# Two copies per tile for the first 24 tiles of the first expert layer, and an order that TensorE no longer reads

## The reference

```python
x = x + _L0_ffn_ref(_L0_cond_ref(x, fside, len, ...), gate_w, gate_b, w1, b1, w2, b2)
x = x + _L1_ffn_ref(_L1_cond_ref(x, W1, b1, v, type), gate_w, w_gate, w_up, w_down, ...)
# _L0_ffn_ref: 24 experts, each token takes its best 2
h = gelu(einsum('bsd,edf->besf', x, w1) + b1)        # 128 -> 512
y = einsum('besf,efd->besd', h, w2) + b2             # 512 -> 128
out = einsum('bse,besd->bsd', combine, y) + x
```

## Time and profile before

| | |
|---|---|
| three runs | 435.76, 437.19, 439.93 us, median 437.19 |
| the profiled execution | 436.51 us, its span 434.7 us, granted TensorE clock 0.942 |
| PE busy | 372.5 us (86%) |
| DVE busy | 281.0 us (65%) |
| ACT busy | 247.2 us (57%) |
| POOL busy | 198.7 us (46%) |
| attention | up to about 176 us |
| first expert layer | 176 to 275 us |
| second layer | 275 us to the end |

### The profile page before, as it was taken

How to read it: one execution, slowest core, us unless ns; L and a number is a source line. 1 busy time by engine, 2 the same in 40 slices (tenths; PEclk the granted TensorE clock), 3 DMA queues, 4 the chain that set the end, 5 groups by cost and what they waited for, 6 DMA issues and landing times.

```text
span 434.7 us, 10203 instructions
## 1 busy us (share of the span) xinstructions
PE 372.5 (86%) x2635; PEld 268.8 (62%) x2635; DVE 281.0 (65%) x1114; ACT 247.2 (57%) x742; POOL 198.7 (46%) x270
## 2 busy tenths in 40 slices
PE   3699999999999995399999899559988879999920
PEld 2356656666666653299999899226556547777710
DVE  3766787887887888366666466369575626666615
ACT  1288888788888783255665456237975114444400
POOL 3551143444433444634454555422747606666630
PEclk9999999999999997599999999759999989999975
DMA  7400999987777703366766676050111122323217
GB/s 153 76 15 13 315 355 228 242 185 165 176 193 188 141 15 98 93 171 177 200 172 182 176 191 193 17 185 15 50 37 44 56 51 78 90 76 82 68 46 248
DMA packets 61072, 57.14 MB, mean 131 GB/s; under 512 B 6042, under 2 KB 49703, under 8 KB 60768
## 3 DMA queue, kind: packets, MB, share of 16 engines
q1 hardware_dynamic: 56288, 48.10, 44.4%
q0 software_dynamic: 4736, 8.47, 5.8%
HBM read 36.12 MB, written 21.73 MB: 133 GB/s over the span
## 4 chain that ended last, share of the span: by engine, by line
PE 70%; DVE 7%; DMA 7%; issue 4%; ACT 3%; POOL 3%; SPq 2%; DVEq 1%; POOLq 0%; ACTq 0%
PE bank L735 13%; PE bank L863 8%; PE bank L1062 7%; PE bank L868 7%; PE bank L744 6%; PE bank L758 5%; PE bank L1079 2%; PE bank L1070 2%; PE bank L1080 2%; DMA w<-in_L_ffn_w_dram 2%; POOL layer_rows L703 2%; DMA qexp<-layer_outputs 2%; PE bank L788 2%; PE bank L774 1%; PE bank L838 1%
## 5 line engine op out<-in xcount | busy, mean ns | idle before, releaser
L1107 ACT ACTIVATE ps<-bank,ntop 128x128 f32<-128x128 f32 x256 | 73.6, 379 | 12.9 <-DVE ntop L1367 12.9
L1174 ACT ACTIVATE hT<-bank,w 128x128 f32<-128x128 f32 x176 | 51.0, 369 | 43.8 <-PE bank L863 43.4
L735 PE MATMUL bank<-qexp 128*128 128x512 f32 x128 | 67.7, 611 | 3.2 <-POOL qexp L645 2.7
L715 POOL DMA_INDIRECT layer_outputs<-w_all x40 | 38.9, 972 | 34.1 <-issue 20.4
L744 PEld LDWEIGHTS bank<-ident,ps 128*128 128x128 f32 x256 | 31.9, 141 | 33.3 <-issue 29.6
L863 PE MATMUL bank<-xT,w 128*128 128x128 f32 x352 | 49.3, 285 | 2.7 <-DMA w<-in_L_ffn_w_dram 1.2
L642 POOL TENSOR_TENSOR qexp<-kA,rowmask 128x512 f32<-128x512 f32 x16 | 16.6, 1039 | 73.2 <-DVE kA L1451 73.2
L1116 ACT ACTIVATE pT<-bank 128x512 f32<-128x512 f32 x64 | 38.6, 603 | 19.7 <-PE bank L744 18.4
L1366 DVE TENSOR_REDUCE mx<-bank 128x4 f32<-128x512 f32 x64 | 43.7, 683 | 7.5 <-PE bank L735 6.2
L863 PEld LDWEIGHTS bank<-xT,w 128*128 128x128 f32 x352 | 44.4, 198 | 4.7 <-issue 3.9
L703 POOL DMA_INDIRECT layer_rows<-rows_all,places x32 | 30.9, 966 | 23.8 <-DVE rows_all L1733 9.4
(11 more groups left out here) (312 smaller groups left out, 811.2 us busy)
## 6 DMA issues: line engine op xcount, KB each, us to landing
w<-in_L_ffn_w_dram SPq DMA_DIRECT2D x44, 258.0 KB, 3.4
layer_rows<-fill SPq DMA_DIRECT2D x10, 910.0 KB, 9.1
w_all<-in_L_ffn_w_dram SPq DMA_DIRECT2D x24, 256.0 KB, 5.1
qexp<-layer_outputs SPq DMA_DIRECT2D x8, 512.0 KB, 4.8
xt<-layer_rows SPq DMA_DIRECT2D x45, 65.0 KB, 2.5
w_all<-layer_rows SPq DMA_DIRECT2D x40, 65.0 KB, 1.8
xfT<-in_xfT_dram SPq DMA_DIRECT2D x16, 128.0 KB, 2.8
layer_rows<-fill SPq DMA_DIRECT2D x1, 1560.0 KB, 11.3
```

Source lines behind the costliest of these rows:

```text
L715: g.indirect_dma_start(ys1_dram, bass.IndirectOffsetOnAxis(ap=xt1[r][:, P:P + 1].bitcast(U32), axis=0), yb1[r][:, :], None, bounds_check=Y ...
L735: pe.matmul(psA[g % 2][:, :], qexp[b % 2][:, g, :], kexp[b % 2].rearrange("p g k -> p (g k)"), start=True, stop=True).then_inc(a_in_ps, 1)
L1107: m = s.activation(ps[g % 2][:, t, :], psA[g % 2][:, t * P:(t + 1) * P], ACT.Exp, bias=ntop[:, h:h + 1])
L1174: s.activation(hT[r % 2][:, c, :], banks[c][:, 0:P], ACT.Gelu, bias=w1[r][:, F0 + c:F0 + c + 1]).then_inc(gelu_done, 1)
```

## The change

DVE now copies w2 and b2 of the first 24 tiles too, with the same `keep_weights`, after take_xT(j+1) and ahead of the rest of iteration j. TensorE reads the four fixed buffers in every tile and loads no order word. DVE loads one word at every fourth tile, inside the loop, in place of all six ahead of it. The wait for all down weights (`w2_in`) moves from TensorE to DVE. In the second layer two waits are added: `pooled_rows(k)` on `pnT_ready`, `keep_pnT(k)` on `pl_in_ps`.

```diff
@@ tensor
-            pe.wait_ge(w2_in, 16 * E0)
-            pe.wait_ge(order_ready, 1)
-            words0 = [order_word(pe, n) for n in range(E0 // RING)]
+            def down_kept(j, r):
+                pe.wait_ge(weights_kept, 2 * j + 1)
+                down(j, r, lambda c: w2_r[r][:, c * P:(c + 1) * P])
+
             transpose_tile(0, 0, 0)
...
-                    down(j - 1, (j - 1) % RING, w2_ordered(j - 1))
+                    down_kept(j - 1, (j - 1) % RING)
...
             def pooled_rows(k):
+                pe.wait_ge(pnT_ready, k + 1)
@@ scalar
             def keep_pnT(k):
                 act.wait_ge(pn_in_ps, k + 1)
                 if k >= 1:
+                    act.wait_ge(pl_in_ps, k)
@@ vector
+            def keep_weights(e, r):
+                v.tensor_copy(w2_r[r], w2_all[:, bass.ds(e, 1), :].rearrange("p o f -> p (o f)")).then_inc(weights_kept, 1)
+                v.tensor_copy(b2_r[r], b2_all[:, bass.ds(e, 1), :].rearrange("p o d -> p (o d)")).then_inc(weights_kept, 1)
+
+            def kept_y(j, r, n):
+                dve.wait_ge(weights_kept, 2 * j + 2)
+                take_y(j, r, n, b2_r[r])
...
-            words0 = [order_word(dve, n) for n in range(E0 // RING)]
+            dve.wait_ge(w2_in, 16 * E0)
             take_xT(0, 0, 0, True)
             for j in range(E0):
                 take_xT(j + 1, (j + 1) % RING, (j + 1) // RING, True)
+                if j % RING == 0:
+                    word = order_word(dve, j // RING)
+                keep_weights(of_order(word, j % RING), j % RING)
                 if j == TABLE_TILE:
                     read_table()
                 if j == TABLE_TILE + 1:
                     gates()
                 if j > 0:
-                    take_y(j - 1, (j - 1) % RING, (j - 1) // RING, b2_ordered(j - 1))
+                    kept_y(j - 1, (j - 1) % RING, (j - 1) // RING)
```

More of the change, by code:

```diff
@@ L908, in _ @@
             extra(0, 0, 0)
-            down(E0 - 1, (E0 - 1) % RING, w2_ordered(E0 - 1))
+            down_kept(E0 - 1, (E0 - 1) % RING)
             for r in range(1, RING):
                 extra(r, r, 0)
-                down_extra(r - 1, r - 1)
+                down_kept(E0 + r - 1, r - 1)
             with pe.Fori(1, nr) as n:
@@ L916, in _ @@
                     extra(j, r, n)
-                    down_extra(j - 1, (r - 1) % RING)
+                    down_kept(E0 + j - 1, (r - 1) % RING)
             pe.wait_ge(y_ready, E0 - 2 + nr * RING)
-            down_extra(nr * RING - 1, RING - 1)
+            down_kept(E0 + nr * RING - 1, RING - 1)
             def turn_x2(k):
@@ L1553, in take_y @@
                 v.tensor_tensor(yb[r][:, :], banks[6 + r % 2][:, 0:P], b2, ALU.add).then_inc(y_ready, 1)
-            def b2_ordered(j):
-                e = of_order(words0[j // RING], j % RING)
-                return b2_all[:, bass.ds(e, 1), :].rearrange("p o d -> p (o d)")
+            def keep_weights(e, r):
[4 more added lines that the diff above has]
+                take_y(j, r, n, b2_r[r])
             def read_table():
@@ L1624, in extra_xT @@
                 take_xT(E0 + 1 + RING * n + r, (r + 1) % RING, n + first_extra + (r + 1) // RING, False)
[L1626 to L1635, removed]
             extra_xT(0, 0)
             word = dve.value_load(round_words[0:1, 0:1], min_val=0, max_val=32 ** RING - 1)
-            keep_weights(word, 0)
-            take_y(E0 - 1, (E0 - 1) % RING, (E0 - 1) // RING, b2_ordered(E0 - 1))
+            keep_weights(of_round(word, 0), 0)
+            kept_y(E0 - 1, (E0 - 1) % RING, (E0 - 1) // RING)
             for r in range(1, RING):
                 extra_xT(0, r)
-                keep_weights(word, r)
-                extra_y(0, r - 1)
+                keep_weights(of_round(word, r), r)
+                kept_y(E0 + r - 1, r - 1, first_extra)
             with dve.Fori(1, nr) as n:
@@ L1646, in _ @@
                 word = round_word(dve, n)
-                keep_weights(word, 0)
-                extra_y(n - 1, RING - 1)
+                keep_weights(of_round(word, 0), 0)
+                kept_y(E0 + RING * n - 1, RING - 1, n - 1 + first_extra)
                 for r in range(1, RING):
                     extra_xT(n, r)
-                    keep_weights(word, r)
-                    extra_y(n, r - 1)
-            extra_y(nr - 1, RING - 1)
+                    keep_weights(of_round(word, r), r)
+                    kept_y(E0 + RING * n + r - 1, r - 1, n + first_extra)
+            kept_y(E0 + RING * nr - 1, RING - 1, nr - 1 + first_extra)
             cx = Chain(chain_x, 1000)
```

## The result

The changed kernel took 435.13 us (median of 20 runs, 433.89 to 436.70), the kernel before, run beside it 20 times, 436.51 (one of these 20 took 1256.66, the others 435.36 to 439.93): a ratio of 0.9968, 95% interval 0.9955 to 0.9981. That is 1.4 us faster, against 1.1 forecast on the profiled execution. The median itself was forecast at 435.8, 0.7 above what came: that forecast went out from the median of three runs of the kernel before, 437.19, which over 20 runs is 436.51. In a later set of runs it was 435.29 against 436.64, 0.9964 (0.9943 to 0.9984). The profiled execution of the changed kernel took 435.33 us, its span 433.5 us (434.7 before).

What follows compares the result with a forecast made beforehand. DVE's six word loads were taken to bound the layer's start, TensorE's 1.90 us pace the ordered tiles; -4.03 + 0.3 + 1.46 + 1.17 = -1.1 us on 436.51 gave 435.4, median forecast 435.8, range 433.0 to 438.5.

Steps and rivals of the forecast that it cites:

- forecast A: Whole kernel: start gained, table and POOL's adds take most of it back, 434.5 to 437 us; chance 0.58.
- Part 1: Layer start: without the word loads the first up-projection starts at 177.33, not 181.36; -4.03 us.
- Part 4: Early tiles: POOL's two unmoved adds hold DVE's weight copies till about 184.9; +1.17 us, bounds 0 and 1.8.
- Part 3: Table, tiles 5 to 8: DVE's added word load and copies delay tile 8's up-projection; +1.46 us, bounds 0.56 and 1.81.
- Part 2: Tiles 8 to 23: with two copies per tile DVE needs 7.54 us per four tiles, TensorE 7.60; +0.3, bounds 0 and +2.8.
- 0.43 at 182.4: Sign in the early tiles: a w2 copy near 182.4 lasting 0.43 us, not over 0.8, would mean rival B.
- rival B: Early tiles and table: adds don't hold the copies, little lost at the table; 433.0 to 434.5 us; chance 0.19.
- the half clock costs nothing here: Early tiles: TensorE's half clock adds 0 us while the adds hold DVE, since TensorE waits anyway.
- Rival C: Ordered tiles: DVE becomes the bound, from 0.08 us a tile of disturbance; slower, 437.9 to 438.6 us; chance 0.18.
- Parts that cost nothing: Ordered tiles and second layer: TensorE's dropped register operations, weight arrival, added waits and POOL's sends change the time by nothing.
- POOL's sends have 0.9 us to spare: POOL's sends follow y and have 0.9 us to spare per tile, so they cost nothing.
- the extras and the second layer don't change their length: Extra tiles and second layer: nothing in them should change their length; a change would show the prediction wrong.

Runs made afterwards that it cites:

- loads moved: Kernel before, without copies in the first 24 tiles, order words loaded inside the loop on DVE and TensorE, one per four tiles: 433.49 us, ratio 0.9928.
- copies alone: Changed kernel with DVE loading all six order words ahead of tile 0 and none in the loop: 436.97 us, ratio 1.0011.
- bias later: Changed kernel with the pool bias steps started three tiles later, the last three done in the first extra round: ratio 0.9957, repeated 434.05 us, ratio 0.9926.
- adds behind the sends: Changed kernel with POOL's first two residual adds moved from before its first send to behind its last send of the layer: 440.02 us, ratio 1.0076.
- adds ahead of the wait: Changed kernel with POOL's two residual adds put ahead of its wait for the last scattered rows: ratio 1.0029, on a slower chip.
- the last experiment: Kernel before, loads in the loop, no copies, bias steps three tiles later, POOL's two adds behind its sends of tiles 10 and 15: 434.81 us, ratio 0.9966.
- all the moves: Kernel before, no copies, loads in the loop, three words loaded behind xT(0), adds before the wait, bias three tiles later: ratio 0.9967, slower chip.
- one copy more: Changed kernel with a third 128x512 copy on DVE in each of ordered tiles 7 to 23, into an unread buffer: 435.69 us, ratio 0.9979.
- the third set: Later runs on one chip of the changed kernel (435.29 us, ratio 0.9964) and variants, beside the kernel before (436.64 us).
- the first experiment: Same run as loads moved: kernel before, no copies in the first 24 tiles, order words loaded in the loop: 433.49 us, ratio 0.9928.

## Why the prediction was right, and where not

The time fell in the forecast A, and the mechanism is shown: the loads' hole is the gain (loads moved, copies alone); DVE round the table takes part of it back (bias later), POOL's adds another (adds behind the sends, adds ahead of the wait). By its steps:

| step | forecast | ledger of the profiles |
|---|---|---|
| Part 1, start | -4.03 | -4.17, of which 0.2 because the attention stage ended earlier in this execution |
| Part 4, adds | +1.17 at tile 8 (1.4 at tile 3) | +1.22 (tiles 0 to 3) |
| Part 3, table (tiles 3 to 8) | +1.46 | +0.95 |
| Part 2, even stretch | +0.3 | +0.51 |
| at tile 23 | -1.1 | -1.49 |

**Part 1** was right in place and size, and in what would be late next, the rows of tile 0. DVE's loads set it, as said: with those alone left, the first up-projection is at 181.17. DVE was nearly the late one itself: its `idx` of tile 0 lasted until 176.76, the transpose until 176.72, so rows that landed sooner would have brought hardly more.

**Part 4** came out right in sum by luck, through two errors. Its own working has a slip: the up-projection of tile 3, 188.84 before, is at 184.81 when shifted by 4.03, not at 184.97, so the lag foretold there is 1.6; it was 1.22. At tile 8 it said 2.63 for both parts, and 2.17 came. The held instructions were others, because the adds move with the landing of the last scattered rows, which I had taken as fixed. I had made "0.43 at 182.4" the mark of rival B; it was seen, and B did not follow. The mark was too narrow: it should have named any DVE operation of these tiles ending with an add. That "the half clock costs nothing here" holds while there is a hold. The clock rose later behind the start than I kept it in the changed kernel (granted 0.80 from 182 to 184 us; from the up-projection of tile 1 to that of tile 2, up(1) to up(2), 3.36 us, 2.89 before), earlier in two others (granted 1.00 from 182 to 184 us; 2.76 with the loads moved, 2.66 with the bias later), and tiles 0 to 3 took 8.70, 8.90 and 8.70 all the same; over the seven profiles with the early start and the adds in their old place they lie between 8.70 and 9.02. Only where the adds are gone does it show: 7.90 and 7.86, with up(1) to up(2) at 3.32 and 3.27, are 0.4 over the 7.48 of before. So of the +1.22 only 0.8 comes back without the adds. The hold itself is seen from up(2) to up(3), 2.65 in the changed kernel, 1.89 with the adds moved.

No run shows the term as it was set up, a weight copy held until 184.9 in these tiles: that POOL's adds would hold a copy as they held `cnt` was my estimate, and the +1.17 rested on it. What the runs showed in its place is DVE operations of three kinds that are longer beside an add: `below`, a small tensor-scalar (0.44 in the changed kernel, 1.13 with the loads moved, 0.23 without adds); operations with two inputs (`under` 1.02 for 0.17, the bias product of the last experiment 2.02 for 0.68); and a weight copy inside SBUF in two other kernels (2.46 for 0.43 with the adds ahead of the wait, 0.80 in tile 0 with the loads at the start). Which of the two engines is the one held when DVE starts first isn't settled by them. In the last experiment the bias product began 0.26 us ahead of the add and was the one that took 2.02, the add 1.20. But the three cases of this kind began inside an indirect DMA issue of POOL's: this one at 206.49, with the issue before the add lasting from 205.75 to 206.73, its like at the second add (1.94, from 217.12, with the issue from 216.31 to 217.28), and `cnt` of the kernel with all the moves at 180.16, with the scatter from 179.77 to 180.74. `cnt` takes 0.18 when nothing holds it, and would then have been over well before the add at 180.77. So DVE may have been waiting since the issue already; against that, the product of 208.89 took 0.67 beside the issue of 208.12, which was itself 1.27 long for 0.98. Without an issue beside it a DVE operation that began first kept its length: in the second layer of the changed kernel the last `qexp` product of four, begun at 283.07, took 0.34 like its fellows, and the add begun at 283.14 took 1.31, where the two of 182.96 took 1.16 each. No run took this apart. What the runs show is that a start ahead of the add, as the profile has it, didn't save those three DVE operations from the hold.

**Part 3** was too dear by 0.5. From xT(5) to the up-projection of tile 8 8.64 us went by (189.75 to 198.39), against 8.9 to 9.1 foretold. A plain tile costs DVE 1.57 and not 1.69: behind xT the weight copy follows by 0.20 (209.67 to 209.87) where I had taken 0.35 from the extras; what makes the difference was not shown. Most of what is left comes from the word loads among the copies: with the loads at the start the table costs 0.38. The adds have no part in it: with them moved away tiles 3 to 8 still took 12.44.

**Part 2** was right that DVE stays under TensorE, on the wrong grounds. Its margin isn't 0.06 us in four tiles but 4 x 0.24 = 0.96 when it never waits (one copy more), and the loss of 0.51 isn't from disturbance: it is the load tile, 2.33 on DVE, whose late xT costs TensorE 0.1 to 0.2 each round. With the loads at the start it is nothing (28.51). Rival C, with its condition of 0.08 a tile, thus had too much of a chance at 0.18; even a whole copy more per tile costs only 1.4 by the ledger, 0.6 by the time.

**"Parts that cost nothing."** For TensorE's register operations, the added waits and the weights this held: the kernel with the copies and DVE's loads at the start has them all and takes as long as the one before. "POOL's sends have 0.9 us to spare" holds for the ordered tiles alone. In the extra tiles POOL is the slower one; changed kernel:

```profile
237.02 0.98 POOL L676 DMA_INDIRECT layer_outputs<-yb,row_r  x1 [0.85 <-POOL row_r L691]
238.01 0.19 POOL L691 COPY row_r<-idx 128x1 uint32 x1
239.06 0.98 POOL L676 DMA_INDIRECT layer_outputs<-yb,row_r  x1 [0.85 <-POOL row_r L691]
```

Send to send is 2.04 us (0.19 + 0.85 + 0.98, and gaps), TensorE needs 1.90. The 20 sends took 41.0 us from first to last before and 40.9 after, though the first up-projection of the extras to the last took 39.64 and 37.78. The layer ends by POOL's chain, which I had not read (changed kernel, its sends of the extras):

```profile
L676 POOL DMA_INDIRECT layer_outputs<-yb,row_r x20: 983/983/1123, 235.0 to 275.9; - x20
```

That the extras and the second layer don't change their length, as the prediction took it, is true of no pair of profiled executions. The extras' up-projections took 37.8 to 40.9 us over fourteen profiles, and in the middle of the second layer the clock sinks in some of them (granted 0.59 from 352 to 358 us in the changed kernel) and not in others (1.00 in the first experiment). A window of the changed kernel, then of the first experiment (last columns: granted clock, DMA share, GB/s):

```profile
352.00:364.00 12.00, 11.87 (x59) 8.83 (x58) 5.83 (x20) 4.91 (x14) 4.37 (x5) 0.80 0.26 68
```

```profile
352.00:364.00 12.00, 11.67 (x69) 8.97 (x69) 6.96 (x23) 5.42 (x17) 5.48 (x6) 1.00 0.32 83
```

The group of matmuls that follows shows what it costs (first and last start; changed kernel, then first experiment):

```profile
L1056 PE MATMUL bank<-wgu,w_all x80: 459/558/948, 348.9 to 411.3; 128*128 x80
```

```profile
L1064 PE MATMUL bank<-wgu,w_all x80: 458/509/559, 349.3 to 409.2; 128*128 x80
```

62.4 us with the clock at 0.80 in the window from 352 to 364, 61.1 with 0.86 (before), 59.9 with 1.00. Against the profile before, the changed one has 2.4 us less at the last send, 2.7 less where this group begins, 1.4 less at its end and 1.2 less in the span. Of this I count the ledger's 1.49 as the change's; what came beyond it between tile 23 and the last send, and went with the clock, isn't traced to it. Both profiles of the changed kernel have the drop (0.80 and 0.79), so that the change itself brings it on isn't excluded. The granted clock averaged over whole executions gives no sign of it: 0.942 on average over the 20 runs of the changed kernel and 0.943 over 12 in the third set, 0.940 and 0.939 over 26 and 23 runs of the kernel before in the first and third. A clock that is back at about 182.8 us (0.80 from 182 to 184) and not at 186.0 gives a difference of 0.004 by itself (an estimate: 3.2 us less at half clock, 3.2 x 0.5 / 434). The second layer by itself was seen in the profiles alone, so that this stays open.

The best of what was tried is the kernel before with its loads in the loop, or the changed kernel with its bias steps three tiles later, 434.3 and 434.1 in one set. The loads in the loop together with the later bias and untouched adds was not run.

## To carry to other kernels

Small serial reads of control words by an engine's own queue were dear ahead of its loop here (4.0 us for DVE's six) and cheap inside it (tiles 8 to 23 took 28.61 us with both engines' loads in their loops and 29.02 with DVE's among its copies, for 28.51): look for them first where an engine idles at a stage's start with "issue" or its queue as the reason. When a stage starts earlier, list what stays where it was (here POOL's adds), what it will now fall on, and any second queue that runs slower than the one you sped up. Judge an engine's spare time by its back-to-back gaps and a test copy, not by the gaps of tiles in which it waits.

## What was not expected of the hardware

- TensorE's six word loads, 3.7 us ahead of its loop, cost next to nothing when one stands in each round (28.61 for 28.51 us in tiles 8 to 23).
- POOL's adds held even DVE operations that began before them (2.02 for 0.68 with 0.26 us of lead, 2.98 for 0.18 with 0.61), both begun inside an indirect DMA issue of POOL's; and one operation was held through two adds in two kernels (2.46, 2.98).
- POOL took 0.85 us from its own small copy of row numbers to the indirect DMA that reads them, so a send with such a copy cost 2.04 us (237.02 to 239.06).
- A weight copy beside an indirect DMA issue of POOL's was stretched further than the 0.58 of the earlier trace rows: 0.71 at 216.94 in the kernel with one copy more, beside the issue from 216.42 to 217.39.
